# Mixture-of-experts tail of a decoder kernel: the shared expert's tile goes first in each group, the routing weights are turned behind its down products

## The reference

```
def swiglu(x, w1, w3, w2): return silu(x @ w1.T) * (x @ w3.T) @ w2.T
x    = layernorm(x).reshape(-1, 128)             # 4096 tokens
w, i = gate(x, w_gate)                           # sigmoid, 2 of 4 groups, 4 of 16 experts, normalised
c    = (one_hot(i, 16) * w[..., None]).sum(1)    # combine weights, token x expert
g, u = silu(einsum('th,efh->tef', x, w1_e)), einsum('th,efh->tef', x, w3_e)
out  = einsum('tef,ehf,te->th', g * u, w2_e, c) + swiglu(x, w1_s, w3_s, w2_s)
```

## Time and profile before

| what | value |
|---|---|
| median of 3 runs | 1340.47 us (1338.61 to 1345.85) |
| profiled execution, own time | 1338.67 us |
| its span, first to last instruction | 1336.9 us |
| TensorE matmuls busy | 1081.8 us (81%) |
| VectorE busy | 985.5 us (74%) |
| ScalarE busy | 806.4 us (60%) |
| GpSimd busy | 568.0 us (42%) |
| mean granted TensorE clock | 0.95 |

### The profile page before, as it was taken

One profiled execution on the slowest core, in us unless ns is written; L12 is line 12 of the kernel. 1 busy time (PEld: TensorE's weight loads), 2 busy tenths in 40 slices (PEclk: granted clock), 3 DMA queues, 4 the chain that ended last, 5 costly groups with the idle time before them and its releaser, 6 DMA issues. The chain is left out here.

```text
span 1336.9 us, 40719 instructions
## 1 busy us (share of the span) xinstructions
PE 1081.8 (81%) x12503; PEld 709.7 (53%) x12503; DVE 985.5 (74%) x3610; ACT 806.4 (60%) x1653; POOL 568.0 (42%) x752
## 2 busy tenths in 40 slices
PE   2688888874888888887698788888887758999998
PEld 0355555552544444444585466656555535666565
DVE  2699999963667676765564499999998648888885
ACT  1498888972777777776132588888876442333331
POOL 4789998932222222221110366666656701111220
PEclk9899999995999999999698899999998878999999
DMA  7000000001000000000121488888887440000000
GB/s 222 14 3 2 0 0 0 1 2 51 15 2 1 0 0 0 0 0 2 56 59 33 111 237 237 234 233 233 234 235 206 114 127 1 16 9 8 8 9 16
DMA packets 170479, 91.28 MB, mean 68 GB/s; under 512 B 8922, under 2 KB 168804, under 8 KB 170132
## 3 DMA queue, kind: packets, MB, share of 16 engines
q1 hardware_dynamic: 169860, 88.05, 24.0%
q0 software_dynamic: 528, 2.10, 0.5%
HBM read 52.11 MB, written 38.01 MB: 67 GB/s over the span
## 5 line engine op out<-in xcount | busy, mean ns | idle before, releaser
L831 POOL TENSOR_TENSOR rr<-ms_eps,minus_half 128x16 f32<-128x16 f32 x64 | 185.7, 2919 | 28.1 <-DVE ms_eps L1048 28.1
L1190 DVE TENSOR_REDUCE rowmax<-psum 128x4 f32<-128x768 f32 x128 | 123.1, 962 | 66.8 <-PE psum L2161 66.8
L559 PE MATMUL psum<-identb,stacks 128*128 128x128 bf16 x1800 | 138.6, 224 | 29.7 <-DVE stacks L1097 12.6
L559 PEld LDWEIGHTS psum<-identb,stacks 128*128 128x128 bf16 x1800 | 111.5, 100 | 60.4 <-issue 23.3
L1394 DVE CUSTOM_DVE_ANT_0 summed<-psum,pos_score 128x128 f32<-128x128 f32 x512 | 117.9, 285 | 25.5 <-PE psum L2361 20.8
L1963 ACT ACTIVATE pos_rows<-psum 128x512 f32<-128x512 f32 x72 | 43.0, 597 | 143.4 <-PE psum L2545 133.8
L2403 PE MATMUL psum<-consts,summed 128*128 128x128 f32 x512 | 84.7, 290 | 43.4 <-DVE summed L1400 41.6
L1849 ACT ACTIVATE probsT<-psum 128x512 f32<-128x512 f32 x128 | 76.5, 598 | 59.1 <-PE psum L654 39.4
L892 POOL TENSOR_TENSOR rest<-staged,stacks 128x128 f32<-128x128 f32 x32 | 13.7, 428 | 216.6 <-ACT stacks L542 216.6
L654 PE MATMUL psum<-probsT,values 128*32 128x128 f32 x2048 | 85.9, 284 | 21.4 <-DVE attn L677 16.6
L383 POOL TENSOR_TENSOR rstd<-vareps,minus_half 128x4 f32 (+1 forms) x16 | 16.9, 1054 | 194.4 <-DVE vareps L374 172.1
(11 more groups left out here) (320 smaller groups left out, 2932.1 us busy)
## 6 DMA issues: line engine op xcount, KB each, us to landing
skew<-pos_rows SPq DMA_DIRECT2D x128, 258.0 KB, 3.8
pos_score<-skew SPq DMA_DIRECT2D x128, 256.0 KB, 4.1
X<-in_x_dram POOLq DMA_DIRECT2D x1, 2048.0 KB, 11.7
ctxT<-in_ctx_dram SPq DMA_DIRECT2D x1, 2048.0 KB, 10.4
yT<-in_ctx_dram SPq DMA_DIRECT2D x32, 64.0 KB, 1.8
ctxT<-in_ctx_dram SPq DMA_DIRECT2D x32, 64.0 KB, 1.8
out_dram<-X SPq DMA_DIRECT2D x8, 256.0 KB, 2.3
pos_rows<-in_ctx_dram SPq DMA_DIRECT2D x25, 64.0 KB, 1.9
```

What stands on the lines that cost most here:

```text
L559: last = pe.transpose(turned[:, t, :], stacks[:, which, 2 * t:2 * t + 2, :].rearrange("s h k -> s (h k)"), identb[:, :])
L831: pool.tensor_tensor(out=rr[:, par, i * H:(i + 1) * H], in0=ms_eps[:, i * H:(i + 1) * H], in1=minus_half[:, 0:H], op=ALU.pow).then_inc(A.r ...
L1190: dve.tensor_reduce(rowmax[:, par, PT * r:PT * r + PT].rearrange("s (h b) -> s b h", b=2), B.max_space, AX.X, ALU.max, negate=True).then_i ...
```

## The change

The shared expert's tile becomes tile 0 of a group and the routed tiles 1 to 8. `weights_of` maps the place to the weights, which lie in memory as before. `spread_weights`, the waits on F.a and VectorE's `tile` shift by one. In TensorE's body, `second_up` of tile 1 and the down products of tile 0 now stand before `turn_combine`, `first_up` of tile 2 stands before `gate`, and the first spread after it. On ScalarE the sigmoid of the gate moves from behind tile 1's silu to behind tile 2's. ROUTE_AT, the layer norm's places, the prologue and the final `down` are unchanged in the code; that final `down` is now a routed tile.

```diff
--- before.py
+++ after.py
@@ -1550,10 +1550,10 @@
                 def tile(g, gpar, k):
 
                     n, par = g * TILES + k, (gpar + k) % 2
-                    routed = g * (TILES - 1) + min(k, TILES - 1)
+                    routed = g * (TILES - 1) + k - 1
                     wait(dve, F.silu, n + 1)
                     wait(dve, F.h3, n + 1)
-                    if k < TILES - 1:
+                    if k > 0:
                         wait(dve, F.a, routed)
                         dve.tensor_tensor(gated[:, :], silu[:, par, :], F.h3_bank[par], ALU.mult).then_inc(F.gated, 1)
                         wait(dve, F.gated, n + 1)
@@ -1969,7 +1969,7 @@
                             save_group(g + 1, 1 - par)
                         if k == 1:
                             save_combine(g, par)
-                        if left >= 1 and k == 1:
+                        if left >= 1 and k == 2:
                             gate(g + 1)
 
                 act.wait_ge(E.x, 1)
@@ -2538,35 +2538,38 @@
                         last = pe.matmul(F.gate_bank[:, k * S:(k + 1) * S], parts3[:, k, :], identb[:, :], start=True, stop=True)
                     last.then_inc(F.cT_ps, 1)
 
+                def weights_of(k):
+
+                    return TILES - 1 if k == 0 else k - 1
+
                 def first_up(g, gpar, k):
                     n, par = g * TILES + k, (gpar + k) % 2
                     x = xT[:, gpar, :, :].rearrange("d b s -> d (b s)")
                     wait(pe, F.silu, n - 1)
-                    pe.matmul(F.h1_bank[par], w_up1[:, k, :], x, start=True, stop=True).then_inc(F.h1, 1)
+                    pe.matmul(F.h1_bank[par], w_up1[:, weights_of(k), :], x, start=True, stop=True).then_inc(F.h1, 1)
 
                 def second_up(g, gpar, k):
                     n, par = g * TILES + k, (gpar + k) % 2
                     x = xT[:, gpar, :, :].rearrange("d b s -> d (b s)")
                     wait(pe, F.gated, n - 1)
-                    pe.matmul(F.h3_bank[par], w_up3[:, k, :], x, start=True, stop=True).then_inc(F.h3, 1)
+                    pe.matmul(F.h3_bank[par], w_up3[:, weights_of(k), :], x, start=True, stop=True).then_inc(F.h3, 1)
 
                 def spread_weights(g, gpar, k):
-                    if k == 0:
+                    if k == 1:
                         wait(pe, F.cT, g + 1)
-                    wait(pe, F.a, g * (TILES - 1) + k)
-                    pe.matmul(F.combine_bank, spreadb[:, k, :], combineT[:, gpar, :, :].rearrange("e b s -> e (b s)"),
+                    wait(pe, F.a, g * (TILES - 1) + k - 1)
+                    pe.matmul(F.combine_bank, spreadb[:, k - 1, :], combineT[:, gpar, :, :].rearrange("e b s -> e (b s)"),
                               start=True, stop=True).then_inc(F.spread, 1)
 
                 def down(g, gpar, k):
                     n, par = g * TILES + k, (gpar + k) % 2
                     if k == 0:
                         wait(pe, F.x, g)
-                    if k < TILES - 1:
-                        wait(pe, F.a, g * (TILES - 1) + k + 1)
+                        wait(pe, F.gated, n + 1)
                     else:
-                        wait(pe, F.gated, n + 1)
+                        wait(pe, F.a, g * (TILES - 1) + k)
                     for b in range(4):
-                        last = pe.matmul(F.y_bank[:, b * D:(b + 1) * D], hidden_a[:, par, b * S:(b + 1) * S], w_down[:, k, :],
+                        last = pe.matmul(F.y_bank[:, b * D:(b + 1) * D], hidden_a[:, par, b * S:(b + 1) * S], w_down[:, weights_of(k), :],
                                          start=(k == 0 and b == 0), stop=(k == TILES - 1 and b == 3), skip_group_check=True)
                     last.then_inc(F.y, 1)
 
@@ -2579,18 +2582,21 @@
                     if left >= 1:
                         turn_group(pe, F, g + 1)
                     first_up(g, par, 1)
+                    second_up(g, par, 1)
+                    down(g, par, 0)
                     turn_combine(g)
-                    second_up(g, par, 1)
-                    spread_weights(g, par, 0)
+                    first_up(g, par, 2)
                     if left >= 1:
                         gate(g + 1, 1 - par)
-                    for k in range(1, TILES):
-                        if k > 1:
-                            first_up(g, par, k)
-                            second_up(g, par, k)
+                    spread_weights(g, par, 1)
+                    second_up(g, par, 2)
+                    down(g, par, 1)
+                    spread_weights(g, par, 2)
+                    for k in range(3, TILES):
+                        first_up(g, par, k)
+                        second_up(g, par, k)
                         down(g, par, k - 1)
-                        if k < TILES - 1:
-                            spread_weights(g, par, k)
+                        spread_weights(g, par, k)
 
                 pe.wait_ge(ld.f, LOADS_F)
                 pe.wait_ge(F.cast, 1)
```

## The result

The changed kernel takes 1346.23 us (median of 12 runs, 1344.28 to 1351.05), the kernel before 1340.08 (12 runs): the ratio is 1.0048, 95% interval 1.0033 to 1.0063. It is 6.15 us slower; 6.0 were forecast. The profiled execution took 1345.79 us, its span is 1344.0 against 1336.9. Of these 7.1 us, 0.71 lie ahead of the cast of group 0's weights (line 1548, at 1107.66 against 1106.95), in code that the change does not touch. From that cast to the start of the last residual the experts take 232.93 us against 226.52, 6.41 more.

A forecast was written before the change was run, and what follows sets the result against it. VectorE, with its front waits, was taken to set the loop groups' period. Terms 2.2 + 0.5 + 3.3 + 0.1 - 0.1 gave 6.0 us slower, 1346.5 us beside the median 1340.47; range 1341.5 to 1350.5.

The forecast's parts named there:

- a(1): Start of tile 1's second VectorE product, after its wait for the spread; forecast at X+6.88, where it was X+6.28.
- X: Start of the last down product of the group before; forecast 0.22 us later in a loop group.
- group 0, cast to the last down product: Group 0: turn waits for tile 0's product behind four VectorE additions, TensorE at half clock; 2.2 us slower.
- group 1: Unrolled group outside the loop: 0.3 for the front and 0.2 for the spread, 0.5 us slower.
- groups 2 to 5: Loop groups: 0.60 us from a later a(1) plus 0.22 from a later X, 0.82 each, 3.3 us in all.
- group 6: Group paced by TensorE: a(1) 0.6 later, one up product less behind it, one spread more; 0.1 us slower.
- group 7 to the last residual: Last group: front 1.1 us faster, final down product 1.15 later, less a spread's 0.22; stated sum -0.1 to 0.
- The last tile: End of a loop group: routed last tile delays the cast 0.88 us counted from a(1), to X+1.69.
- The front: Start of a loop group: turn queues behind tile 0's down products, starting at X+4.25; a(1) 0.60 us later.
- VectorE sets the period: Loop groups: VectorE's stream, 23.42 us without waits from a(1) to the cast, plus its front waits, sets the period.
- The table loads: ScalarE's function loads of 1.28 us around the gate's sigmoid, now behind tile 2's silu, stay covered by other work.
- faster rival: Tile 0 without weights covers their way round, a(1) before X+5.5; 7.0 us faster, 1333.5 us; chance 0.07.

The follow-up runs named there:

- fastest version: Changed kernel with turn between tile 1's up products, first spread before tile 0's down products, gate after tile 1's down products, groups 2 to 5 written out: 1331.57 us.
- unrolled version: Changed kernel with groups 2 to 5 written out instead of looped on VectorE, ScalarE and TensorE: 1342.55 us.
- more on VectorE: Changed kernel with one additional VectorE addition (128x512, unused buffers) behind tile 4 in groups 0 to 6: 1353.66 us.
- turn early: Changed kernel with only the turn of the weights moved ahead, between the two up products of tile 1, in all groups: 1343.53 us.
- group 0's turn early: Changed kernel with the turn ahead of tile 0's down products in group 0 alone: 1346.26 us.

## Why the prediction was right

The mechanism is the one forecast, and for the groups of the loop the experiments show it: take the turn out from behind the down products, or the gate out of the chain, and a(1) comes earlier by about the slots that the prediction gave them; give VectorE more to do and the period grows by it. For group 0 the number is in part luck.

Each term of the sum beside the profile. The periods of X are 27.81, 29.09, 28.67, 28.87, 28.67 and 27.35 us before, 28.39, 29.66, 29.34, 29.93, 29.34 and 27.45 after, for groups 1 to 6.

| term | forecast | measured |
|---|---|---|
| group 0, cast to the last down product | 2.2 | 32.24 - 29.62 = 2.62 |
| group 1 | 0.5 | 0.58 |
| groups 2 to 5 | 3.3 | 0.57 + 0.67 + 1.06 + 0.67 = 2.97 |
| group 6 | 0.1 | 0.10 |
| group 7 to the last residual | -0.1 | 26.58 - 26.44 = 0.14 |
| sum | 6.0 | 6.41 |

**The last tile.** Forecast: the cast at X+1.69, X itself 2.93 behind the down product of tile 7. Measured 1.70 and 2.93. From a(1) to the cast 24.31 us, which is 23.42 + 0.89.

**The front.** Forecast and measured behind X: product 2.52 and 2.53, down products 3.26 and 3.27, turn 4.25 and 4.26, gate 5.39 and 5.43, a(1) 6.88 and 6.73. The stretch from the gate to a(1) was too long by 0.19, the gate itself came 0.04 later than forecast: I put its eight weight loads and the load of the spread end to end. Removing it from the chain gave back 0.89 us and moving the turn 0.39. The long single wait of VectorE is 2.63 in group 5, forecast 2.9.

**VectorE sets the period.** Shown by the additional work, which lengthened groups 1 to 5 by its time less what the neighbouring step gave back. That is shown for the changed kernel. In the fastest version TensorE seems to set it.

**The table loads** are covered, as forecast: the sigmoid of 1264.73 follows its load of 1263.43 by 0.02, and the second load ends at 1266.25, before the silu of tile 3 has its h1. The drain that the Trainium skill adds ("ScalarE: Activation LUTs", section "What ACT_TABLE_LOAD costs") shows in neither kernel.

**Not seen.** The stall ahead of group 4's residual. The prediction read only group 5, where it does not occur, and took four equal groups. The 0.4 us that it cost in group 4 was balanced by the shorter gate. That the sum came out within 0.4 us rests in part on such balancing.

**The end and group 0.** The final pair of down products cost 2.10 - 0.89 = 1.21, forecast 1.15. From X to the down products of tile 7, group 7 gave back 24.25 - 23.28 = 0.97, forecast 1.1 and 0.2. The prediction's own terms for this group sum to -0.17, not to the -0.1 to 0 that it states.

Group 0 was 0.4 dearer in this pair of traces: full clock came at 1120.5, where I had 1119 and the group began 0.7 later. The forecast let the clock take as long as in the kernel before, some 9 us behind the start of work. It did so here (9.5) and in the unrolled version (8.8), where the term is 31.89 - 29.62 = 2.27, but not in "more on VectorE" (4.3). There the same order took 30.91, less an estimated 0.39 for the addition, which leaves a loss of 0.9. So the term of 2.2 is the size of two traces out of three, and what the prediction took as its rule for the clock is not borne out.

The faster rival's condition, a turn free of VectorE's product and a(1) before X+5.5, was met only by the versions that move turn and spread; the first of them was 4.8 us faster than the kernel before in the same comparison (1335.46 and 1340.21).

## What to carry to other kernels

Putting work that needs no late value first hides the value's latency only if the instructions that bring the value are not themselves queued behind that work. When a tile moves to another place, count what the place's neighbours now wait for: here the last tile lengthened the routing's stream by 0.88 us while the first shortened a wait that came back one tile later. Read more than one instance of a loop body: a stall in one of them can lie under a wait that the change is about to remove. Before you put a difference in one group down to an edit, look for another kernel with the same code in that group: here the same code took 33.48 and 31.97 us.

## What the runs showed of the hardware

In a loop, a dependent VectorE product that waits on its predecessor starts 0.86 to 0.88 us after it, in straight code with constant counts 0.70 to 0.73 (up to 0.79 in the kernel before, unrolled). The residual of the loop's first body comes 0.45 us late in the second pass and 0.16 in the first. In all, the loop cost 4.1 to 4.6 us in four groups. Unrolled code has stalls of its own: groups of 28.6 beside 28.3. Where these stalls come from, no run tells.

VectorE's two comparisons over 1024 columns take 2.49 us together ahead of group 0, where GpSimd is idle, and in the loop's groups 1.22 for the first and 2.12 for the second, which overlaps a GpSimd operation by 1.04 us; 1.90 where the overlap is 0.82. The other way round, that GpSimd operation took 2.74 us instead of 2.35 beside an addition of VectorE. That the two engines hinder each other is stated in the Trainium skill ("Advanced Engine Details and Errata", section "Mode Summary") for VectorE's two-port modes; whether that is the mechanism here, no run tells.

From one profiled execution to another, the same code ahead of the experts ended up to 7.8 us apart (1105.9 to 1113.7). Behind 7 to 10 us without work for TensorE, the clock rose to full between 4.3 us (work set in at 1116.36) and 12.2 us (at 1113.60) after work had set in, and one order of the same instructions showed both 4.3 and 9.5. With the same code, group 0 took 33.48 us in "turn early" and 31.97 in "group 0's turn early".
